# Attention, grouped convolution and low-rank experts on one core: row tiles for the mixing weights, a new order of the first steps, new shapes for mask, feed-forward and lora

## The reference

```python
# 1. conditional 1x1 mixing of the 32 tokens, weights mixed from 8 experts by the condition
h   = gelu(gelu(cond @ W0 + b0) @ W1 + b1)
att = softmax(h @ W2 + b2)                                  # (128, 8)
agg_w = einsum('bk,koi->boi', att, weight); agg_b = att @ bias_k
y   = einsum('boi,bih->boh', agg_w, x) + agg_b[:, :, None]
# 2. causal attention with rope: 32 query heads, 8 key heads, head size 16; residual
x   = x + attention(y, Wq, Wk, Wv, Wo)
# 3. grouped convolution over the features (9 taps, 4 groups) plus a condition term
z   = conv1d(x, L0_cond2_weight, groups=4, pad=4) + (cond @ c_weight.T)[:, :, None] + fside
# 4. feed-forward: dense 512x512, router over 15 logits, 8 experts of rank 16; residual
w   = top8 of softmax(z @ router_W.T + router_b), summed by expert_map
lora = einsum('bter,eor->bto', (z @ A.T) * w, B) * 2
out = x + z @ base_W.T + base_b + lora
```

## Time and profile before

| | |
|---|---|
| median of 3 runs | 631.05 us (629.39 to 631.32) |
| profiled execution | 629.44 us, of which the span of the instructions 627.5 us |
| PE busy in the span | 600.0 us (96%) |
| DVE busy | 475.9 us (76%) |
| ACT, POOL busy | 226.6 us, 224.4 us (36% each) |
| DMA | 71.23 MB, mean 114 GB/s |

### The profile page before, as it was taken

How to read it: one execution, slowest core, us unless ns; L and a number is a source line. 1 busy time by engine, 2 the same in 40 slices (tenths; PEclk the granted TensorE clock), 3 DMA queues, 4 the chain that set the end, 5 groups by cost and what they waited for, 6 DMA issues and landing times.

```text
span 627.5 us, 14234 instructions
## 1 busy us (share of the span) xinstructions
PE 600.0 (96%) x4928; PEld 500.8 (80%) x4928; DVE 475.9 (76%) x1201; ACT 226.6 (36%) x635; POOL 224.4 (36%) x181
## 2 busy tenths in 40 slices
PE   5988899999999999999999999999999999999886
PEld 3676778888888888888888888888888888888764
DVE  3567857778887877787878777788787778787753
ACT  4263333334333333333333333343344333333320
POOL 7164233233334433334344332333443323334310
PEclk9989989999999999999999999999999999999999
DMA  7824624444554344445653444455533444554430
GB/s 177 189 76 109 138 84 109 101 115 118 130 130 126 99 93 111 109 112 130 130 125 104 95 109 107 109 130 130 130 109 94 111 95 110 130 130 109 107 87 35
DMA packets 125190, 71.23 MB, mean 114 GB/s; under 512 B 48773, under 2 KB 107301, under 8 KB 125048
## 3 DMA queue, kind: packets, MB, share of 16 engines
q1 hardware_dynamic: 123696, 70.53, 47.1%
q10 hardware_dynamic: 1336, 0.24, 0.2%
q0 software_dynamic: 144, 0.28, 0.2%
HBM read 51.49 MB, written 19.53 MB: 113 GB/s over the span
## 4 chain that ended last, share of the span: by engine, by line
PE 80%; DMA 9%; DVE 4%; SPq 3%; issue 2%; ACT 1%; ACTq 0%; DVEq 0%
PE ps L415 17%; PE ps L566 15%; PE ps L593 8%; PE ps L587 7%; DMA scratch<-x_dram 7%; PE ps L613 5%; PE ps L605 5%; PE ps L515 4%; PE ps L552 4%; PE ps L632 3%; PE ps L654 3%; PE ps L621 2%; PE ps L577 2%; PE ps L555 1%; PE ps L601 1%
## 5 line engine op out<-in xcount | busy, mean ns | idle before, releaser
L941 POOL TENSOR_TENSOR qk<-network,t 128x640 f32<-128x640 f32 x31 | 48.1, 1551 | 160.1 <-DVE t L1118 160.1
L415 PE MATMUL ps<-wqkv_hi,y_hi 128*128 128x512 f32 (+1 forms) x256 | 87.3, 341 | 0.8 <-POOL y_lo L931 0.8
L415 PE MATMUL ps<-wqkv_hi,y_lo 128*128 128x512 f32 (+1 forms) x256 | 87.1, 340 | 0.0
L415 PE MATMUL ps<-wqkv_lo,y_hi 128*128 128x512 f32 (+1 forms) x256 | 86.9, 340 | 0.0
L953 POOL TENSOR_TENSOR raw<-x1p,basebB 128x512 f32<-128x512 f32 x32 | 49.4, 1545 | 54.4 <-DVE x1p L1195 54.4
L743 ACT ACTIVATE raw<-ps 128x512 f32<-128x512 f32 x64 | 37.7, 594 | 71.4 <-PE ps L632 71.3
L948 POOL TENSOR_TENSOR raw<-raw,zero 128x512 f32<-128x512 f32 x32 | 33.3, 1039 | 83.6 <-DVE raw L1184 83.6
L964 DVE TENSOR_TENSOR oT_lo<-ps,oT_hi 128x256 fp32r<-128x256 f32 x64 | 24.2, 420 | 48.1 <-ACT oT_hi L743 48.1
L805 ACT ACTIVATE raw<-raw 128x512 f32<-128x512 f32 x64 | 40.4, 632 | 52.8 <-DVE raw L1137 52.8
L925 POOL TENSOR_TENSOR raw<-raw,rz 128x512 f32<-128x512 f32 x32 | 33.6, 1050 | 63.2 <-DVE rz L1147 63.2
L415 PEld LDWEIGHTS ps<-wqkv_hi,y_hi 128*128 128x128 f32 x256 | 48.7, 190 | 8.3 <-issue 1.5
(11 more groups left out here) (182 smaller groups left out, 1483.2 us busy)
## 6 DMA issues: line engine op xcount, KB each, us to landing
scratch<-x_dram SPq DMA_DIRECT2D x96, 256.0 KB, 5.8
x_dram<-x1p SPq DMA_DIRECT2D x32, 260.0 KB, 2.1
xm<-x SPq DMA_DIRECT2D x32, 256.0 KB, 4.6
xr<-x SPq DMA_DIRECT2D x32, 256.0 KB, 2.6
out<-raw SPq DMA_DIRECT2D x32, 256.0 KB, 2.1
v_dram<-vS SPq DMA_DIRECT2D x32, 64.0 KB
vB<-v_dram SPq DMA_DIRECT2D x128, 16.0 KB, 4.9
mixb<-mixb_dram SPq DMA_DIRECT2D x28, 64.0 KB, 3.8
```

The lines of the kernel that those rows point to most:

```text
L415: last = mm(dst, a, b, start=(n == 0), stop=(n == 3 * len(left) - 1))
L941: nc.gpsimd.tensor_tensor(qk[:, :], t1, t2[:, :], ALU.add).then_inc(qk_sb, 1)
```

## The change

- `BASE6` is 256 instead of 384: the product L587 gets 400 columns instead of 272, L593 gets 256 instead of 384; lora is twice three matmuls of 256 columns instead of three of 384 and three of 128; the additions of DVE (L1091, L1182, L1184) take 256 columns each.
- The mask matmuls take 64 rows (the added 32 of the stationary block are zero).
- Half of `oT_hi` is copied by DVE, half by ACT; `project` waits for both.
- `mixing_weights` uses two row tiles: attention weights transposed into rows 0 to 7 and 32 to 39, `cwI` likewise; the experts' weights are loaded twice for that.
- `mix(0)` stands ahead of the bias products. `prepare_ar` goes behind the first transposes of q and k; `prepare_base((0, 1))` goes behind the first transposes of p, into banks 6 and 5.
- Loads: A and router ahead of B; group 1 of x ahead of the bias store; baseW waits for the mixing weights of groups 1 to 3; the mixing weights of groups 4 to 31 are loaded as soon as their store has landed, before step 0 of SP.

```diff
-BASE6 = 3 * P
+BASE6 = 2 * P
...
-        cwI = scratch[0:NCOND, S * S:2 * S * S].rearrange("k (i o) -> k i o", i=S)
+        cwI = scratch[0:S + NCOND, S * S:S * S + S * S // 2].rearrange("k (i o) -> k i o", i=S // 2)
...
+        attP = sb("attP", [P, 2, S])
+        attT = sb("attT", [2 * S, P])
...
+        def base_bank(j):
+
+            return (6, 5, 6, 7)[j]
...
+            sp.dma_start(rawA, loraA.rearrange("e r l -> (e r) l")).then_inc(ld["A"], 16)
+            sp.dma_start(rawR[0:NR, :], routerW).then_inc(ld["R"], 16)
             for j in range(PH):
                 sp.dma_start(rawB[:, j, :, :], loraB.rearrange("e (p j) r -> j p e r", j=PH)[j]).then_inc(ld["B"], 16)
-            sp.dma_start(rawA, loraA.rearrange("e r l -> (e r) l")).then_inc(ld["A"], 16)
-            sp.dma_start(rawR[0:NR, :], routerW).then_inc(ld["R"], 16)
+            sp.wait_ge(y_ps, 1)
+            sp.dma_start(xm[:, :], group(x_g, 1)).then_inc(xm_in, 16)
             sp.wait_ge(aggb_sb, 1)
             sp.dma_start(mixb_dram, aggb[:, :]).then_inc(aggb_dram, 16)
...
-            sp.wait_ge(y_ps, 1)
-            sp.dma_start(xm[:, :], group(x_g, 1)).then_inc(xm_in, 16)
             sp.wait_ge(aggb_dram, 16)
             sp.dma_start(mixb[:, P:4 * P], mixb_row[P:4 * P].partition_broadcast(P)).then_inc(mixb_in, 16)
+            sp.wait_ge(mixw_in2, 16 * NB)
             sp.dma_start(rawbase, baseW.rearrange("(p j) l -> p j l", j=PH)).then_inc(ld["base"], 16)
...
+            sp.wait_ge(mixw_out, 16)
+            load_mixw(sp, 4, G, mixw_in)
...
-                if peeled(t, 1):
-                    sp.wait_ge(mixw_out, 16)
-                    load_mixw(sp, 4, G, mixw_in)
...
-            nc.tensor.transpose(ps[0:NCOND, 0, 0:P], att, ident).then_inc(attT_ps, 1)
-            pe.wait_ge(attT_sb, 1)
-            pe.wait_ge(ld["cbias"], 16)
-            mm(ps[:, 2, 0:S], attT[:, :], cbiasS[:, :], start=True, stop=True).then_inc(aggb_ps, 1)
-            pe.wait_ge(biasR_sb, 1)
-            pe.wait_ge(ones_sb, 1)
-            mm(ps[:, 3, 0:P], ones8, biasR, start=True, stop=True).then_inc(mixb0_ps, 1)
+            nc.tensor.transpose(ps[0:2 * S, 0, 0:P], attP[:, :, :].rearrange("p h k -> p (h k)"), ident).then_inc(attT_ps, 1)
+
+            def first_bias():
+
+                pe.wait_ge(biasR_sb, 1)
+                pe.wait_ge(ones_sb, 1)
+                mm(ps[:, 3, 0:P], ones8, biasR, start=True, stop=True).then_inc(mixb0_ps, 1)
+                pe.wait_ge(attT_sb, 1)
+                pe.wait_ge(ld["cbias"], 16)
+                mm(ps[:, 4, 0:S], attT[0:NCOND, :], cbiasS[:, :], start=True, stop=True).then_inc(aggb_ps, 1)
 
             def mixing_weights():
 
-                pe.wait_ge(cwI_sb, 1)
+                pe.wait_ge(cwI_sb, 2)
                 for h in range(2):
-                    mm(ps[:, 6 + h, :], attT[:, :], cwI[:, S // 2 * h:S // 2 * (h + 1), :].rearrange("k i o -> k (i o)"),
+                    rows = slice(S * h, S * h + NCOND)
+                    mm(ps[:, 6 + h, :], attT[rows, :], cwI[rows, :, :].rearrange("k i o -> k (i o)"),
                        start=True, stop=True).then_inc(aggw_ps, 1)
...
-                    last = mm(ps[:, 2, 0:P], a[:, :], b[:, BASE6:D], start=(n == 0), stop=(n == 2))
+                    last = mm(ps[:, 2, 0:D - BASE6], a[:, :], b[:, BASE6:D], start=(n == 0), stop=(n == 2))
...
                 pe.wait_ge(oT_hi_sb, u + 1)
+                pe.wait_ge(oT_hi_dve, u + 1)
...
-                    rows = slice(h * P // 2, h * P // 2 + S)
+                    rows = slice(h * P // 2, (h + 1) * P // 2)
                     mm(ps[:, h, :], query16[rows, :], causal16[rows, :], start=True, stop=False)
...
             def steps(t):
+                if peeled(t, 1):
+                    pe.wait_ge(base_lo_sb, 2)
                 if live(t):
                     transpose_qk(t)
+                if peeled(t, 0):
+                    prepare_ar()
                 if peeled(t, 2):
                     pe.wait_ge(base_lo_sb, PH)
...
-                    pe.wait_ge(aggb_sb, 1)
...
                     mix(t + 1)
                 if peeled(t, -1):
+                    first_bias()
                     mixing_weights()
...
-                if peeled(t, 0):
-                    pe.wait_ge(prep_sb, 1)
-                    prepare_base((0, 1))
...
                     prepare_conv()
-                    prepare_ar()
...
                     transpose_p(t)
+                if peeled(t, 0):
+                    pe.wait_ge(prep_sb, 1)
+                    prepare_base((0, 1))
...
-            act.dma_start(cwS[:, :, :], cweight.rearrange("k o i a -> k o (i a)")).then_inc(ld["cw"], 16)
+            for h in range(2):
+                act.dma_start(cwS[S * h:S * h + NCOND, :, :], cweight.rearrange("k o i a -> k o (i a)")).then_inc(ld["cw"], 16)
...
-                    for a in range(2):
-                        last = copy(heads(oT_hi, a), heads_ps(a))
-                    last.then_inc(oT_hi_sb, 1)
+                    copy(heads(oT_hi, 0), heads_ps(0)).then_inc(oT_hi_sb, 1)
+                if peeled(t, 0):
+                    prepare_base((0, 1))
...
-            v.tensor_scalar(att, attE, attR, None, ALU.mult).then_inc(att_sb, 1)
+            v.tensor_scalar(attP[:, :, 0:NCOND], attE.unsqueeze(1).broadcast_to([P, 2, NCOND]), attR, None, ALU.mult
+                            ).then_inc(att_sb, 1)
...
-                v.tensor_tensor(x1b[:, 3, :], ps[:, 7, 0:P], x1b[:, 3, :], ALU.add).then_inc(last_sb, 1)
+                v.tensor_tensor(x1b[:, 2:4, :], ps[:, 7, 0:D - BASE6].rearrange("p (j n) -> p j n", j=2), x1b[:, 2:4, :], ALU.add).then_inc(last_sb, 1)
...
+                dve.wait_ge(o_ps, t + 1)
+                v.tensor_copy(heads(oT_hi, 1), heads_ps(1)).then_inc(oT_hi_dve, 1)
                 dve.wait_ge(oT_hi_sb, t + 1)
-                for a in range(2):
-                    last = minus(heads(oT_lo, a), heads_ps(a), heads(oT_hi, a))
-                last.then_inc(oT_lo_sb, 1)
+                minus(heads(oT_lo, 0), heads_ps(0), heads(oT_hi, 0))
+                dve.wait_ge(oT_hi_dve, t + 1)
+                minus(heads(oT_lo, 1), heads_ps(1), heads(oT_hi, 1)).then_inc(oT_lo_sb, 1)
...
                     prepare_q(0)
+                    prepare_q(2)
+                    first_mixing_bias()
                     dve.wait_ge(mixb0_sb, 1)
                 if peeled(t, 0):
-                    prepare_ar()
                     dve.wait_ge(mixb_in, 16)
                 if live(t + 1):
                     next_y(t + 1)
+                if peeled(t, 0):
+                    prepare_ar()
                 if peeled(t, -1):
-                    prepare_q(2)
+                    keep_bias()
                     first_y_lo()
...
-                if peeled(t, 0):
-                    prepare_base((0, 1))
...
                     low_oT(t)
+                if peeled(t, 0):
+                    prepare_base((0, 1))
```

More of the change, by code:

```diff
@@ L164, in build @@
         cbiasS = sb("cbiasS", [NCOND, S])
[L165 removed]
+        cwS = sb("cwS", [S + NCOND, S, S])
         fsideS = sb("fsideS", [1, S])
@@ L467, in prepare_base @@
                     for jo in range(PH):
-                        last = nc.tensor.transpose(ps[:, 6 + j % 2, jo * P:(jo + 1) * P],
+                        last = nc.tensor.transpose(ps[:, base_bank(j), jo * P:(jo + 1) * P],
                                                    rawbase[:, jo, :].rearrange("o (p j) -> o j p", j=PH)[:, j, :],
@@ L586, in feed_forward @@
                 for n, (a, b) in enumerate(terms):
-                    last = mm(ps[:, 7, 0:P + NAR], a, b[:, BASE6:D + NAR], start=(n == 0), stop=(n == len(terms) - 1))
+                    last = mm(ps[:, 7, 0:D - BASE6 + NAR], a, b[:, BASE6:D + NAR], start=(n == 0), stop=(n == len(terms) - 1))
                 last.then_inc(ar_ps, 1)
@@ L788, in prepare_base @@
                     act.wait_ge(baseT_ps, j + 1)
-                    copy(base_hi[:, j, :], ps[:, 6 + j % 2, :]).then_inc(base_hi_sb, 1)
+                    copy(base_hi[:, j, :], ps[:, base_bank(j), :]).then_inc(base_hi_sb, 1)
             def prepare_lora():
@@ L852, in steps @@
                     act.wait_ge(ar_ps, t - 1)
-                    copy(arS[:, :], ps[:, 7, P:P + NAR]).then_inc(ar_sb, 1)
+                    copy(arS[:, :], ps[:, 7, D - BASE6:D - BASE6 + NAR]).then_inc(ar_sb, 1)
                 if live(t):
@@ L888, in _ @@
             nc.gpsimd.memset(mixw[:, :, :, :], 0.0).then_inc(mixw_zero, 1)
-            pool.wait_ge(ld["cw"], 16)
-            nc.gpsimd.tensor_copy(cwI, cwS[:, :, :].rearrange("k o i -> k i o")).then_inc(cwI_sb, 1)
+            pool.wait_ge(ld["cw"], 32)
+            pool.wait_ge(mixw_zero, 1)
+            for h in range(2):
+                rows = slice(S * h, S * h + NCOND)
+                nc.gpsimd.tensor_copy(cwI[rows, :, :], cwS[rows, :, S // 2 * h:S // 2 * (h + 1)].rearrange("k o i -> k i o")
+                                      ).then_inc(cwI_sb, 1)
```

(10 more changed lines are left out.)

19 lines of the change are left out of this document (5 added, 14 removed).

## The result

The changed kernel takes 615.31 us (median of 4 runs, 614.89 to 615.57), the kernel before 631.18 beside it (629.39 to 631.73): ratio 0.9753, 95% interval 0.9733 to 0.9773. The profiled execution took 615.38 us.

What follows compares the result with a forecast made beforehand. TensorE, busy 96% of the span, sets the pace. Loop -7.1, start -2.1, step 0 -0.3, step 1 +0.7, step 2 -5.0, end +1.1 sum to -12.7 us: 616.7 profiled, 618.3 by median; range 614.5 to 622.

Steps and rivals of the forecast that it cites:

- Lora, `oT_hi`, `project`: In the loop: lora 0.10 us shorter, `project`'s first four matmuls 0.07 by dividing the `oT_hi` copy; 0.17 a step.
- Mask: In the loop, ahead of the convolution: 64 rows leave out one shape change, 0.10 us gained in 23 of 28 steps.
- The upper bound of 8.7: Most that the 28 loop steps were to gain, in us; forecast 7.1, lower bound 2.8.
- Start: From the start to `mix(1)`, put at 28.1: 2.1 us gained, bounds 1.0 and 3.2.
- Step 0: -0.3 us, from DVE's `oT_hi` copy shortening the wait ahead of `project`; clock gain 2.1 or loss 1.7 not taken.
- Step 1: +0.7 us: moved mixing-weight loads cost 1 us through a later `conv(0)` (bounds 0 and 4), less 0.3.
- Step 2: 5.0 us gained, bounds 3.4 and 5.3: without the loads, `conv(1)`'s wait and the low clock behind it go.
- End: Last two steps: +1.1 us, bounds 0.4 and 1.6; later `hw` +1.7, earlier output -0.4, step 31 -0.2.
- B: Loop gives only what lora's columns show; mask and `project` keep their holes: 622.6 us, chance 0.14.
- C: Moved loads make `conv(0)` 4 us late, and PE's clock falls or stays low in step 0: 623.0 us, chance 0.12.
- E: DVE becomes the loop if copies side by side lengthen each other; 632.3 us at 0.5 over, chance 0.05.
- D: Clock holds through `mix(1)` and scores, nothing late in step 1, start at its bound: 614.1 us, chance 0.09.

Runs made afterwards that it cites:

- the two undoings together: Changed kernel with output columns split at 384 again and both `oT_hi` copies on ACT again: 619.9 us, ratio 0.9816 to the kernel before.
- the nine with this code: Nine profiled executions, the changed kernel's and edited ones, with the same code up to `mix(1)`, which starts at 27.7 to 29.0 us in them.
- the repeat: The changed kernel timed once more without any edit: 614.8 us (6 runs), ratio 0.9742 to the kernel before.
- the split of the last two steps: Changed kernel with A and router products computed first, in their own bank, in the last two feed-forwards: 614.6 us, ratio 0.9738.

## Why the prediction was right

Forecast 618.3 us, measured 615.3; in the profiled executions' spans -12.7 forecast and -13.9 measured. Of the 3.0 us between forecast and measurement about 1.4 are in the terms below (629.44 to 615.38 is 14.1 for 12.7). The other 1.6 are the last step of the sum: it added them to get from the profiled execution to the median, and the changed kernel's profiled execution lies at its median.

- Lora, `oT_hi`, `project`: 0.17 us a step forecast; 0.17 by the two undoings together. That lora alone would only become a wait for the copies is shown by the undone copies (17.72). Within the step lora gave 0.11 and `project` 0.07, and the convolution's piece is 0.05 longer in the new shapes (it is short again with the old ones). I had put the 256-column addition of DVE at nothing there, and the rows do not show what lengthens the piece; it stays open.
- Mask: 0.10 a step forecast, 0.20 measured; 23 x 0.10 = 2.3 us in the loop forecast, 4.3 by the undoing. This is the term that was clearly mis-sized: the 0.10 of one change of shape came at the mask, and as much again came at the scores behind it, for which the sum had no term. The steps that wait for `xc` lost nothing net, since the waits are 1.3 us before and 1.4 after. So the loop gave 28 x 0.30 = 8.4 for 7.1; lora, `project` and mask alone would make 28 x 0.38 = 10.6, and the longer piece of the convolution and small differences take 2.2 back. The upper bound of 8.7 was too low by its own parts: with 0.20 for each of the two it is 28 x 0.20 + 23 x 0.20 = 10.2.
- Start: -1.6 for -2.1, in one profile; the nine with this code give -1.2 to -2.5. The queries did come at 17.3, as forecast. The row tiles gave 1.4 us on PE where 1.9 was forecast, but their second load and copy pushed GpSimd's memsets onto DVE's chain, 0.8 us that had no term. The 0.4 that I had charged for ACT's queue was 0.1: the first gelu starts at 5.51 instead of 5.42. Together the row tiles show no gain at `mix(1)`, as far as the one run without them tells. What gained there is then the order of biases, loads and `prepare_ar`; only the biases were undone by themselves, so their shares stay open.
- Step 0: -0.3 as forecast, but by another way. From `mix(1)` to the queries it is 4.55 us instead of 6.19, since `mix(1)` and scores ran at full clock: 1.6 gained. From the queries to the transposes of p it is 5.83 instead of 4.44, since the clock was low there: 1.4 lost. The forecast had named both and taken neither; its 0.3 was to come from the wait ahead of `project`, which fell from 0.90 to 0.75. That the number fits is luck; the repeat took 1.1 less.
- Step 1: I had charged 1 us for the moved loads; they cost nothing that shows. The 0.3 that mask, lora and copy should give does not show either: step 1 takes 15.84 in both profiles, `conv(0)` waits 0.32 us in it now, and its scatter is as large. Step 2: -4.8 for -5.0, and the undoing gives it back.
- End: +1.2 for +1.1; undoing the shapes takes 1.4 off it, the split of the last two steps 1.2. The wait for `hw` in the last step is 1.98 us for a forecast of about 1.9.

Of the rivals, B is refuted (mask and `project` did lose their holes). Of C the late `conv(0)` is refuted, but its other half, a low clock in step 0, did occur and cost 1.4 us there. E is refuted: the copies side by side took 0.42 us on DVE and 0.38 on ACT, what the forecast had, and the convolution waits no more for `xc` than before. The measured time lies between the forecast and D; of D the clock held through `mix(1)` and scores as it said and then fell behind them, and step 1 came true.

## What to carry to other kernels

Two holes that end at the same instant must be closed together, so price an edit with its neighbour's finish time beside it; each alone showed next to nothing here (0 and 0.03 us, together 0.17). When a matmul changes its tile shape, look also at the products behind it: half of the mask's gain lay there. A start-up chain across four engines pays in small places: take from it only what a second profile of the same kernel repeats, and look up the granted clock of both before you set one beside the other.

## What the runs showed that I had not expected

- DVE's operations of 128x16 and 128x128 took 0.97 to 1.28 and 0.84 to 1.14 us while GpSimd's memsets ran, and 0.22 and 0.34 when these stood elsewhere. The first ended with GpSimd's memsets (11.83 us, the memset of `cvR` at 11.78). The Trainium skill (SBUF — State Buffer, "Who interferes with whom") has VectorE and GpSimd share one pair of ports, held for a whole instruction, and names tensor_scalar among the operations that can want it; the ends in the trace agree. That the operation is held until the end of `cvR`, over more than one memset, is more than the rule tells, and no run here explains it. In the kernel before, the memset of `cvR` ended at 10.82 us, just ahead of these operations.
- The granted clock may fall or hold over the same idle stretch of 2.2 us of the same program. It fell in some executions and held in others at two places, step 0 and step 31, and where it fell the stretch took 1 to 3 us more: as much as most of the edits above are worth.
- SP issued the same four loads in 2.09 us at one place and in 4.14 at another, where they had other DMAs close in front of and behind them. What makes the difference was not tested.
